# Layer 1 head sums, their fp16 parts and their transposed copies in two buffers each, in a two-layer graph attention kernel

## The reference

```
# layer 0
h  = relu(layernorm(x))
m  = h @ map_w.T + map_b                       # 8 heads of 64
n  = m / |m| per head;  gate = (n @ n.T > 0.1), masked by adj
q, k = m @ q_w.T + q_b, m @ k_w.T + k_b
p  = softmax(q @ k.T / 8, masked)              # per head
a  = gate * p
x  = x + relu((a @ (h @ gcn_map_w.T + b)) @ gcn_W.T / (a.sum(-1) + 1))
# layer 1
h  = relu(layernorm(x))
q, k, v = h @ Wq, h @ Wk, h @ Wv               # 4 heads of 64
o  = softmax(q @ k.T / 8, masked by adj) @ v   # [128, 256], the "layer 1 sums"
x  = x + o @ Wo + bo
```

## Time and profile before

| what | value |
|---|---|
| three runs, median (lowest to highest) | 2636.19 us (2632.74 to 2638.48) |
| the profiled execution, its own time | 2636.84 us |
| its span, first to last instruction | 2635.0 us |
| granted TensorE clock, mean over the span | 0.987 |
| PE / PE weight loads / DVE / ACT / POOL busy | 97% / 78% / 78% / 65% / 82% |
| DMA engines busy, hardware queue | 57.5% |

### The profile page before, as it was taken

One profiled execution on the slowest core, in us unless ns is written; L12 is line 12 of the kernel. 1 busy time (PEld: TensorE's weight loads), 2 busy tenths in 40 slices (PEclk: granted clock), 3 DMA queues, 4 the chain that ended last, 5 costly groups with the idle time before them and its releaser, 6 DMA issues.

```text
span 2635.0 us, 78823 instructions
## 1 busy us (share of the span) xinstructions
PE 2558.4 (97%) x30681; PEld 2057.2 (78%) x30681; DVE 2061.8 (78%) x3465; ACT 1708.8 (65%) x4509; POOL 2168.2 (82%) x2452
## 2 busy tenths in 40 slices
PE   6899999999999999999999999999999999999985
PEld 4678888887887877887888788787788878878863
DVE  6478888888878788788878888878887887888873
ACT  3366676676676667667667667666766766766762
POOL 2488888888888888888888888888888888888873
PEclk8999999999999999999999999999999999999997
DMA  5146665665665665666566556556656655655643
GB/s 134 45 85 112 124 121 112 120 125 112 113 126 108 118 120 114 113 123 116 116 119 126 114 113 126 111 115 120 117 112 122 124 108 119 128 108 115 118 95 73
DMA packets 830708, 299.08 MB, mean 113 GB/s; under 512 B 772609, under 2 KB 780289, under 8 KB 830337
## 3 DMA queue, kind: packets, MB, share of 16 engines
q1 hardware_dynamic: 830336, 294.04, 57.5%
HBM read 75.80 MB, written 33.55 MB: 42 GB/s over the span
## 4 chain that ended last, share of the span: by engine, by line
PE 90%; DVE 3%; POOL 2%; ACT 2%; issue 1%; DMA 1%; SPq 0%; DVEq 0%; POOLq 0%; ACTq 0%
PE unit_ps L1376 49%; PE unit_ps L1384 24%; PE s_ps L1394 4%; PE s_ps L1434 3%; PE c_ps L1394 3%; PE unit_ps L1453 2%; PE unit_ps L1468 2%; PE unit_ps L1394 2%; PE unit_ps L1444 1%; DVE qk_hl L992 1%; DMA o_t<-o_hl 1%; ACT e_ec L727 1%; POOL inv_norm L630 1%; DMA h_t<-h_hl 0%; ACT qk_hl L816 0%
## 5 line engine op out<-in xcount | busy, mean ns | idle before, releaser
L727 ACT ACTIVATE e_ec<-e_ec,neg_mx 128x128 f32<-128x128 f32 x1024 | 396.0, 388 | 4.2
L1376 PE MATMUL unit_ps<-h_t,w_m_hi 128*128 128x256 f16 x2048 | 343.2, 275 | 12.8 <-DMA h_t<-h_hl 12.8
L1376 PE MATMUL unit_ps<-h_t,w_q_hi 128*128 128x256 f16 x2048 | 345.0, 274 | 2.7 <-DVE bias_q L1243 2.7
L1376 PE MATMUL unit_ps<-h_t,w_k_hi 128*128 128x256 f16 x2048 | 345.3, 274 | 0.0
L1384 PE MATMUL unit_ps<-w_v_hi,h_t 128*128 128x512 f16 x1024 | 324.9, 379 | 0.0
L581 POOL TENSOR_TENSOR e_ec<-e_ec 128x1024 f16<-128x1024 f32 x128 | 290.7, 2271 | 13.5 <-ACT e_ec L754 13.5
L1376 PE MATMUL unit_ps<-h_t,w_m_lo 128*128 128x256 f16 x1024 | 280.8, 274 | 0.0
L1376 PE MATMUL unit_ps<-h_t,w_k_lo 128*128 128x256 f16 x1024 | 280.5, 274 | 0.0
L1376 PE MATMUL unit_ps<-h_t,w_q_lo 128*128 128x256 f16 x1024 | 280.1, 274 | 0.0
L992 DVE TENSOR_TENSOR qk_hl<-qk_sb,qk_hl 128x512 f16<-128x512 f32 x128 | 169.5, 1324 | 126.4 <-ACT qk_hl L816 126.4
L1376 PEld LDWEIGHTS unit_ps<-h_t,w_m_hi 128*128 128x128 f16 x2048 | 196.4, 98 | 42.5 <-issue 13.4
(11 more groups left out here) (197 smaller groups left out, 7702.6 us busy)
## 6 DMA issues: line engine op xcount, KB each, us to landing
xa<-in_x_dram SPq DMA_DIRECT2D x128, 256.0 KB, 3.7
xres<-in_x_dram SPq DMA_DIRECT2D x128, 256.0 KB, 2.8
out_dram<-ybuf SPq DMA_DIRECT2D x128, 256.0 KB, 2.5
h_t<-h_hl SPq DMA_TRANSPOSE x256, 3.2
ec_t<-e_ec SPq DMA_TRANSPOSE x256, 3.2
adj_in<-in_adj_dram SPq DMA_DIRECT2D x128, 16.0 KB, 2.1
p_t<-p_hl SPq DMA_TRANSPOSE x128, 3.3
o_t<-o_hl SPq DMA_TRANSPOSE x128, 3.8
```

Source lines behind the costliest of these rows:

```text
L727: ins = nc.scalar.activation(e[:, h, :], e[:, h, :], ACT.Exp, bias=neg[:, h:h + 1], scale=SCALE, accum_out=sums[:, h:h + 1])
L1376: ins = nc.tensor.matmul(out, w[a][:, i, c * P:(c + 1) * P], h[:, :, b, i, :], start=n == 0, stop=n == len(passes) - 1)
```

## The change

The scaled sums, their two parts and the turned parts get a second buffer, picked by the parity of the graph; so do the reciprocals. The landing of a transpose is signalled on one of two semaphores. `o1_upper` of a graph now waits only for the landing of the graph two before it, `o1_rows` for the lower part of the graph two before, and `turn_o1` for the output product of two slots before. No instruction is added or taken away but for waits, and no order is changed.

```diff
-        o1_sb = sb("o1_sb", [P, INNER])
-        o_hl = sb("o_hl", [P, 2, INNER], F16)
-        o_t = sb("o_t", [P, 2, C1, P], F16)
+        o1_sb = sb("o1_sb", [P, 2, INNER])
+        o_hl = sb("o_hl", [P, 2, 2, INNER], F16)
+        o_t = sb("o_t", [P, 2, 2, C1, P], F16)
...
-        inv_lsum = sb("inv_lsum", [P, H1])
+        inv_lsum = sb("inv_lsum", [P, 2, H1])
...
-        o1_in = sem("o1_in")
+        o1_in = [sem(f"o1_in{i}") for i in range(2)]
...
                     sp.wait_ge(o1_lo, s.at(lambda t: t - 5 + 1))
                     settle(sp, settled_sp, s.i)
-                    if s.has(-6):
-                        sp.wait_ge(unit_full, s.unit("wo", back=1).full)
+                    if s.has(-7):
+                        sp.wait_ge(unit_full, s.unit("wo", back=2).full)
                     settle(sp, settled_sp, s.i)
-                    sp.dma_start_transpose(o_t[:, :, :, :].rearrange("p s c n -> p (s c) n"),
-                                           o_hl[:, :, :].rearrange("p s n -> p (s n)")).then_inc(o1_in, 16)
+                    b = (s.n - 5) % 2
+                    sp.dma_start_transpose(o_t[:, b].rearrange("p s c n -> p (s c) n"),
+                                           o_hl[:, b].rearrange("p s n -> p (s n)")).then_inc(o1_in[b], 16)
...
                     pool.wait_ge(o1_hi, s.at(lambda t: t - behind + 1))
-                    nc.gpsimd.tensor_tensor(o_hl[:, 1, :], o1_sb[:, :], o_hl[:, 0, :], ALU.subtract).then_inc(o1_lo, 1)
+                    b = (s.n - behind) % 2
+                    nc.gpsimd.tensor_tensor(o_hl[:, b, 1, :], o1_sb[:, b, :], o_hl[:, b, 0, :], ALU.subtract).then_inc(o1_lo, 1)
...
                     act.wait_ge(unit_out[u.bank], u.before + 1)
-                    wait(act, o1_in, s.at(lambda t: 16 * (t - behind)))
-                    nc.scalar.activation(o_hl[:, 0, :], o1_sb[:, :], ACT.Copy).then_inc(o1_hi, 1)
+                    b = (s.n - behind) % 2
+                    wait(act, o1_in[b], s.at(lambda t: 16 * ((t - behind) // 2)))
+                    nc.scalar.activation(o_hl[:, b, 0, :], o1_sb[:, b, :], ACT.Copy).then_inc(o1_hi, 1)
...
                     dve.wait_ge(unit_full, u.full)
-                    wait(dve, o1_lo, s.at(lambda t: t - behind))
+                    wait(dve, o1_lo, s.at(lambda t: t - behind - 1))
...
-                    pe.wait_ge(o1_in, s.at(lambda t: 16 * (t - 5 + 1)))
+                    b = (s.n - 5) % 2
+                    pe.wait_ge(o1_in[b], s.at(lambda t: 16 * ((t - 5) // 2 + 1)))
...
-                    rows(ps, w_o, o_t).then_inc(unit_full, 1)
+                    rows(ps, w_o, o_t[:, b]).then_inc(unit_full, 1)
```

More of the change, by code:

```diff
@@ L1037, in o1_rows @@
                     dve.wait_ge(unit_full, u.full)
-                    wait(dve, o1_lo, s.at(lambda t: t - behind))
+                    wait(dve, o1_lo, s.at(lambda t: t - behind - 1))
                     o1 = unit_ps[:, u.bank, 0:H1 * (DH + 1)].rearrange("p (h d) -> p h d", h=H1)
-                    nc.vector.reciprocal(inv_lsum[:, :], o1[:, :, DH]).then_inc(inv_lsum_done, 1)
+                    inverse = inv_lsum[:, (s.n - behind) % 2, :]
+                    nc.vector.reciprocal(inverse, o1[:, :, DH]).then_inc(inv_lsum_done, 1)
                     dve.wait_ge(inv_lsum_done, s.at(lambda t: t - behind + 1))
                     nc.vector.tensor_tensor(
-                        o1_sb[:, :].rearrange("p (h d) -> p h d", h=H1), o1[:, :, 0:DH],
-                        inv_lsum[:, :].unsqueeze(2).broadcast_to([P, H1, DH]), ALU.mult).then_inc(unit_out[u.bank], 1)
+                        o1_sb[:, (s.n - behind) % 2, :].rearrange("p (h d) -> p h d", h=H1), o1[:, :, 0:DH],
+                        inverse.unsqueeze(2).broadcast_to([P, H1, DH]), ALU.mult).then_inc(unit_out[u.bank], 1)
             def norm_sums(s):
```

## The result

The changed kernel takes 2644.21 us (median of 7 runs, 2639.44 to 2645.76) against 2636.19 us before: ratio 1.0027, 95% interval 1.0016 to 1.0039. It is slower by about the amount forecast (2643.2 us, 0.26%). The profiled execution took 2642.43 us, with a span of 2640.6 us.

What follows compares the result with a forecast made beforehand. PE work bounds the kernel, 38.78 us a pair. 58 x 0.28 = 16.2 us lost, 9.3 won back from long pairs: +6.97, so 2643.8 us profiled, 2643.2 predicted (0.26% more); range 2633 to 2648 us.

Steps and rivals of the forecast that it cites:

- The floor: Pair of graphs (odd slot to odd slot), all PE work without a gap: 38.78 us; 9.55 us of 59 pairs lie over it.
- The late pairs: Seven pairs where `k_lower(0)` came just behind POOL's `e_lower`, 1.27 us over each; all go, gaining 8.9 us.
- The early `k_lower(0)`: On DVE without ACT's wait, it starts about 1.2 us earlier, 0.14 to 0.23 behind POOL's first copy (L636).
- The price of 0.28 us a pair: `k_lower(0)` delays POOL's second copy by 0.46 us, so PE's second four transposes come late; bounds 0 to 0.46.
- The slack: Between the end of POOL's two copies and the start of PE's second four transposes: 0.29 us.
- The parts costed at nothing: Second buffers and reciprocals by parity, SP's wait, DVE's wait, and the run's beginning and end: 0 us.
- The sum: 59 pairs at 39.06 us are 2304.54 us against 2297.57: +6.97 us.
- The faster one: Rival: copies not hit, `k_lower(0)` over 0.56 us behind the first; all 59 pairs 38.78, 2626.6 us; chance 0.12.
- the pair at 2488.39: Near the run's end, ACT's wait only 0.68 us: the changed kernel in small, `k_lower(0)` meets the copy; takes 39.06 us.
- The mixed one: Rival: only some pairs have `k_lower(0)` meet the copies, 34 of 59 being even; 2631 to 2641 us; chance 0.16.
- The lock in full: Rival: loser of DVE and POOL's clash always stands the whole instruction; pair 39.32 us, 2658.5 us; chance 0.04.
- the new wait: Sign: PE waits about 0.2 us in each odd slot at L1453 for POOL inv_rows, 59 times or more.

Runs made afterwards that it cites:

- e1: Changed kernel plus one VectorE wait: the first k lower part of an odd slot waits for GpSimd's first copy to inv_rows; 2626.34 us, ratio 0.9968.
- e6: Kernel before, single buffers, ScalarE's second upper part of the sums moved behind the layer 1 q upper part, plus e1's wait; 2625.59 us, ratio 0.9954.
- e7: Changed kernel plus a VectorE wait: the first k lower part waits for GpSimd's second copy to inv_rows; 2626.55 us, ratio 0.9960.
- e4: Changed kernel, with VectorE's first k lower part waiting until GpSimd's second q lower part is done; one run, 2704.77 us.
- e3: Kernel before, single buffers and all waits, ScalarE's second upper part of the sums moved behind the k and layer 1 q upper parts; 2643.12 us, ratio 1.0028.
- e8: Changed kernel, with the first k lower part replaced by a one-input VectorE multiply by zero; one run, 2624.85 us.
- e2: Changed kernel with all second buffers, but ScalarE's upper part of the sums again waits for the landing of the graph right before; 2637.82 us, ratio 1.0013.

## Why the prediction was right, step by step

**The floor and what lies over it.** Right. e1, e6 and e7 put all 59 pairs at the floor, and take 9 to 11 us off the time of before; 9.55 was the forecast for it.

**The late pairs.** Right in cause and size: all seven are gone in the changed kernel, and e4 makes them in every pair.

**The early `k_lower(0)`.** Right: forecast 0.14 to 0.23 behind the first copy, measured 0.14 to 0.15 in 58 of 60 pairs (0.07 and 0.32 in the other two). The price of 0.28 us a pair held in each; e3 has it without the change, and e1 takes it away inside the change. One sentence was too strong: before, DVE did have a two-input instruction during the first copy in one full pair, that of the earlier trace rows, as the prediction itself says further down.

**The slack.** The forecast took the price of 0.28 from a measured pair, and that was right. The slack beside it was not: 0.29, counted to the fifth matmul, would have left 0.46 - 0.29 = 0.17 a pair, some 6.5 us less in all. What waits for the copy is the weight load ahead of that matmul, whose slack is 0.13 (e8).

**The parts costed at nothing.** The second buffers, SP's wait and DVE's wait cost nothing in the pairs that e2, and e1 beside e6, can tell, but for the 1.3 us that e2 leaves open. The end is as forecast: from the last full pair to the end of the span 2635.0 - 2488.39 = 146.6 us before and 2640.6 - 2494.14 = 146.5 us after.

**The sum.** +7.18 us in the pairs against +6.97. The span grew by only 5.6 us, since the third odd slot came 1.4 us sooner (189.39 against 190.82). No step of mine covers that. In the traces of the eight experiments this start lies between 186.5 and 189.7 us, whatever was edited, so I take it for a spread of the beginning, in which weights are loaded and made; the runs do not show its cause.

**The rivals.** The faster one needed `k_lower(0)` to start more than 0.56 us behind the first copy, some 0.4 later than the pair at 2488.39 shows; it did not in any pair (0.32 at most), and e1 shows that it would have paid as computed (2626.6 us forecast, 2626.34 measured). The mixed one fails, as no pair is at 38.78. The lock in full would have given 39.32 us a pair and is ruled out by 39.06.

**How it shows.** I had looked for the new wait, of about 0.2 us, among the rows of PE; it is among those of the weight loads, 0.30 us each.

## What to carry to other kernels

A wait on an engine with idle time can still be holding an instruction away from one that it must not meet. Before taking such a wait away, find what now starts earlier behind it, and what the neighbouring engine is doing at that moment; then look through the trace for a stretch in which it happened by chance (the last pairs, with less work around them, are a good place), and read the price there. If the price is a meeting on the shared SBUF access of VectorE and GpSimd, choose the order at that place with a semaphore: here one wait turned a loss of 8 us into a gain of 9, and a change of order together with the same wait did it without any second buffer (e6).

## What the runs showed of the hardware

Alone, `k_lower(0)` takes 0.69 us (the one that overlaps no GpSimd instruction). When it starts while a GpSimd copy or subtraction runs, 0.15 us or more before that ends, it does not end a full 0.69 us behind it but 0.54 to 0.55 (e1: the copies end at 1288.33, the k lower part at 1288.88). The same holds the other way: the q lower part of e1, 1.16 us alone, ends 1.01 us behind the k lower part, and the second copy, 0.61 alone, 0.47 behind it. So behind the other's end, the one that stood needs some 0.14 us less than its own time.

When it started makes no difference: started 0.07, 0.15, 0.32 or 0.45 us behind the first copy (changed kernel, e3, and the pair of the earlier trace rows), `k_lower(0)` takes 1.09, 1.01, 0.83 or 0.70 us and ends at 1.15 to 1.16 each time, and the two copies take 1.62 to 1.63 each time. If the two had shared the access, the time of overlap would count. The order of their starts settles who goes first: in each of the 59 pairs `k_lower(0)` starts before the second copy and is done before it, and in the late pairs of before `e_lower` starts 0.03 us or more ahead of `k_lower(0)` and goes first.

The Trainium skill (SBUF — State Buffer, "Who interferes with whom") has the loser blocked for the whole instruction. These runs agree that the two do not share; that the 0.14 us are work which the loser does before it needs the access fits them, but no run shows it. The same section says that `tensor_scalar` in the two-port mode excludes GpSimd too. e8 agrees, with 0.74 us against 0.39 and a second copy that again ends 0.47 behind the multiply; that the multiply ran in this mode is taken from its short time and not shown otherwise.
